# Ternarising the weights in steps of 2048 columns with bf16 intermediates instead of 512 columns with f32

## The chip, the cores and the metric

The kernel runs on all 8 NeuronCores of one Trainium2 chip. Each core computes one sequence of a batch of eight, with the same program and its own copy of the weight preparation; the cores exchange nothing. The metric is the device time of the slowest core in microseconds. Engine names as in the profile: PE is TensorE, DVE VectorE, ACT ScalarE, POOL GpSimd, SP the engine that here only issues loads.

## What is computed

One layer of a "sandwich" network on x of shape (8, 4096, 2048), f32: linear attention with 16 heads and 4 key/value heads, then a feed-forward block with ternary weights (BitLinear 1.58).

```python
def weight_quant(w):
    scale = 1.0 / jnp.clip(jnp.mean(jnp.abs(w)), 1e-05)
    q = jnp.clip(jnp.round(w * scale), -1.0, 1.0) / scale
    return w + jax.lax.stop_gradient(q - w)
def bitlinear158(x, w, b):
    xq = act_quant(rms_norm(x))
    wq = weight_quant(w)
    return jnp.einsum('bsd,od->bso', xq, wq) + b

x = x + _layernorm(attn(_layernorm(x), Wq, bq, Wk, bk, Wv, bv, Wo))
# ffn: w1 is (8192, 2048), w2 is (2048, 8192)
#   h = layer_norm(gelu(silu(bitlinear158(x, w1, b1)))); bitlinear158(h, w2, b2)
x = x + _layernorm(ffn(_layernorm(x), w1, b1, ln_g, ln_b, w2, b2))
```

The part that matters here is `weight_quant`: each element of w1 and w2 becomes -1, 0 or 1 once it is multiplied by the scale and rounded, and the scale needs the mean of |w| over the whole matrix first.

## The kernel before

The program is a list of operations per engine, written out by hand; semaphores order them. `vo`, `so`, `po` append an operation to VectorE, ScalarE and GpSimd, `vs` one that also waits for the VectorE operation before it. `dma(queue, ...)` (L157 to L164; the profile puts issues down to L162) appends a transfer to the queue of SP ("sync"), ACT ("scalar") or POOL ("gpsimd"). Each queue has a ring of semaphores, six for SP and three each for ACT and POOL, and a transfer waits until the one that used its semaphore before has landed.

It has two parts. The token loop (from L446) works on 8 tiles of 512 tokens: attention passes over all tiles and then the feed-forward block. The weight preparation in front of it casts the attention weights to bf16, and then handles w1 and w2 one after the other (`for wi, wsrc` at L330), each in two passes over chunks of 128 rows of the transposed matrix:

- The first pass (L333 to L346) loads each chunk to `xf` and sums the absolute values on VectorE. From the sum follows the scale, as a column `swc` (L347 to L365).
- The second pass (L367 to L410), the ternarisation, loads each chunk again and compares: `v_u` (L378) is 1 where w times scale is over 0.5, `v_w` (L384) is 1 where it is under -0.5, and `v_q` (L389) is the difference, in bf16. Then the chunk is stored to HBM, from where the token loop reads it.

A chunk of w1 has 8192 columns and fills all of `xf`: 16 chunks, each load waiting until VectorE is done with the chunk before. It is stored with one transfer of 2 MB to `wq1d` on ACT's queue. A chunk of w2 has 2048 columns, and two halves of `xf` alternate: 64 chunks, so that a load can be issued two chunks ahead. It is stored as 16 pieces of 128 columns to `wq2d`, 8 on ACT's queue and 8 on POOL's. The result buffer is `yb` for even chunks and `sqs` for odd ones, and the first `v_q` of a chunk waits for the last six stores of the chunk two before it (`st_prev`).

The inner loop of the second pass takes 512 columns at a time. `tA(0)` and `tA(1)` are the halves of `tmpA`, 512 f32 columns each; `rot_auxp` makes each comparison wait for the subtraction that last read its half. `xb1` is a bf16 buffer of 8192 columns which the preparation doesn't use; the token loop does. The load of the first tokens waits for all stores of the preparation (`pre_store`).

Of the kernel before, what the change touches and what calls it, by code (L numbers as in the profile page):

```python
# [63 lines left out]
def build_nc(debug=False):  # L64
# [37 lines left out]
    with es:  # L102
        A1 = SB("A1", [128, 32768], BF16)
        A2 = SB("A2", [128, 16384], BF16)
        xf = SB("xf", [128, DC * T], F32)
        yb = SB("yb", [128, DC * T], BF16)
        sqs = SB("sqs", [128, DC * T], BF16)
        xb1 = SB("xb1", [128, DC * T], BF16)
# [77 lines left out]
        vo = lambda fn, waits=(), inc=None: sch.op("vector", fn, waits, inc)  # L186
# [12 lines left out]
        tA = lambda i: tmpA[:, (i % 2) * 512:(i % 2) * 512 + 512]  # L199
        tB = lambda i: tmpB[:, 0:512]  # L200
        aux = lambda i: aux32[:, (i % 2) * 512:(i % 2) * 512 + 512]
        chunk = lambda t, c, w=512: t[:, c * w:(c + 1) * w]
# [34 lines left out]
        def bcast(rowslice, bank, dest, bf16, row_w=()):  # L237
# [7 lines left out]
            else:  # L245
# [30 lines left out]
           waits=[c_bk, c0])  # L276
# [4 lines left out]
                   waits=[W("v", vlast)] + qlast("sync"))  # L281
        slast2 = 0
        for c in range(DC):
            if c % 2 == 0:
                vlast = vo(lambda e, c=c: e.tensor_copy(out=chunk(A2, c),
                                                        in_=chunk(xf, c)),
                           waits=[c_wk] if c == 0 else (),
                           inc="v" if c >= DC - 2 else None)
            else:
                slast2 = so(lambda e, c=c: e.copy(out=chunk(A2, c),  # L290
                                                  in_=chunk(xf, c)),
                            waits=[c_wk] if c == 1 else (),
                            inc="s" if c >= DC - 2 else None)
        c_wv = dma("sync", xf[:].rearrange("p (c o) -> p c o", c=16), wvT.rearrange("(c p) o -> p c o", p=128),
                   waits=[W("v", vlast), W("s", slast2)])
        for c in range(DC):
            if c % 2 == 0:
                vlast = vo(lambda e, c=c: e.tensor_copy(
                    out=A2[:, 8192 + c * 512:8192 + (c + 1) * 512],
                    in_=chunk(xf, c)),  # L300
                    waits=[c_wv] if c == 0 else (),
                    inc="v" if c >= DC - 2 else None)
            else:
                slast2 = so(lambda e, c=c: e.copy(
                    out=A2[:, 8192 + c * 512:8192 + (c + 1) * 512],
                    in_=chunk(xf, c)),
                    waits=[c_wv] if c == 1 else (),
                    inc="s" if c >= DC - 2 else None)
        slast = sch.at("s")
        vlast = sch.at("v")  # L310
        for q4 in range(4):
            src = wqT[q4 * 512:(q4 + 1) * 512, :].rearrange("(c p) o -> p c o",
                                                            p=128)
            c_l = dma("sync", xf[:].rearrange("p (c o) -> p c o", c=4), src, waits=[W("v", vlast), W("s", slast)])
            for c in range(4):
                dc = q4 * 4 + c
                if c % 2 == 0:
                    vlast = vo(lambda e, dc=dc, c=c: e.tensor_copy(
                        out=A1[:, dc * 2048:(dc + 1) * 2048],
                        in_=xf[:, c * 2048:(c + 1) * 2048]),  # L320
                        waits=[c_l], inc="v")
                else:
                    slast = so(lambda e, dc=dc, c=c: e.copy(
                        out=A1[:, dc * 2048:(dc + 1) * 2048],
                        in_=xf[:, c * 2048:(c + 1) * 2048]),
                        waits=[c_l], inc="s")

        rot_auxp = Rot(2)
        rot_wst = Rot(2)
        for wi, wsrc in enumerate((w1T, w2T)):  # L330
            nch = DC if wi == 0 else MC
            wid = HID if wi == 0 else D
            for ch in range(nch):  # L333
                off = 0 if wid == HID else (ch % 2) * 4096
                c_l = dma("sync", xf[:, off:off + wid], wsrc[ch * 128:(ch + 1) * 128, :],
                          waits=(rot_wst.wait(ch) if wid != HID else
                                 [W("v", sch.at("v"))]) +
                                ([W("v", sch.at("v")), W("s", sch.at("s"))]
                                 if ch < 2 else []))
                vs(lambda e, wid=wid, off=off: e.reduce_sum(  # L340
                    out=wacc[:, 2:3], in_=xf[:, off:off + wid], axis=AX.X,
                    apply_absolute_value=True), waits=[c_l])
                va = vs(lambda e, wi=wi: e.tensor_tensor(  # L343
                    out=wacc[:, wi:wi + 1], in0=wacc[:, wi:wi + 1],
                    in1=wacc[:, 2:3], op=OP.add))
                rot_wst.done(ch, "v", va)  # L346
            t_tp = tpose(psp[0:1, 0:128], wacc[:, wi:wi + 1], idf[:],  # L347
                         waits=[W("v", sch.at("v"))] + guard(psp), inc="pe")
            vs(lambda e: e.tensor_reduce(out=wrow[0:1, 0:1], in_=psp[0:1, 0:128],
                                         axis=AX.X, op=OP.add),  # L350
               waits=[W("pe", t_tp)])
            vs(lambda e: e.tensor_scalar(out=wrow[0:1, 1:2], in0=wrow[0:1, 0:1],
                                         scalar1=1.0 / float(D * HID), scalar2=1e-5,
                                         op0=OP.mult, op1=OP.max))
            vs(lambda e: e.reciprocal(out=wrow[0:1, 2:3], in_=wrow[0:1, 1:2]))
            v_sw = vs(lambda e, wi=wi: e.tensor_scalar(
                out=wrow[0:1, 4 + wi:5 + wi], in0=wrow[0:1, 1:2],
                scalar1=1.0 / 127.0, scalar2=None, op0=OP.mult))
            consumed(psp, "v", v_sw)
            t_bc = mm(psp[:, 0:1], onesrf[0:1, :], wrow[0:1, 2:3], True, True,  # L360
                      waits=[W("v", v_sw)] + guard(psp), inc="pe")
            v_swc = vs(lambda e, wi=wi: e.tensor_copy(out=swc[:, wi:wi + 1],
                                                      in_=psp[:, 0:1]),
                       waits=[W("pe", t_bc)])
            consumed(psp, "v", v_swc)  # L365
            st_prev = {0: [], 1: []}
            for ch in range(nch):  # L367
                off = 0 if wid == HID else (ch % 2) * 4096
                wbuf = yb if ch % 2 == 0 else sqs
                c_l = dma("sync", xf[:, off:off + wid],  # L370
                          wsrc[ch * 128:(ch + 1) * 128, :],
                          waits=(rot_wst.wait(ch) if wid != HID else
                                 [W("v", sch.at("v"))]) +
                                ([W("v", sch.at("v"))] if ch < 2 else []) +
                                (qlast("scalar") + qlast("gpsimd")
                                 if ch < 2 else []))
                for j in range(wid // 512):
                    v_u = vo(lambda e, j=j, wi=wi, off=off: e.tensor_scalar(  # L378
                        out=tA(0), in0=xf[:, off + j * 512:off + (j + 1) * 512],
                        scalar1=swc[:, wi:wi + 1],  # L380
                        scalar2=0.5, op0=OP.mult, op1=OP.is_gt),
                        waits=([c_l] if j == 0 else []) + rot_auxp.wait(0),
                        inc="v")
                    v_w = vo(lambda e, j=j, wi=wi, off=off: e.tensor_scalar(  # L384
                        out=tA(1), in0=xf[:, off + j * 512:off + (j + 1) * 512],
                        scalar1=swc[:, wi:wi + 1],
                        scalar2=-0.5, op0=OP.mult, op1=OP.is_lt),
                        waits=rot_auxp.wait(1), inc="v")
                    v_q = vo(lambda e, j=j, wbuf=wbuf: e.tensor_tensor(  # L389
                        out=chunk(wbuf, j), in0=tA(0), in1=tA(1), op=OP.subtract),  # L390
                        waits=[W("v", v_w)] +
                              (st_prev[ch % 2] if j == 0 else []), inc="v")
                    rot_auxp.done(0, "v", v_q)
                    rot_auxp.done(1, "v", v_q)
                m_v = sch.at("v")
                if wid != HID:
                    rot_wst.done(ch, "v", m_v)
                if wi == 0:
                    st_prev[ch % 2] = [dma("scalar",
                                           wq1d[ch * 128:(ch + 1) * 128, :],  # L400
                                           wbuf[:, 0:HID],
                                           waits=[W("v", m_v)])]
                else:
                    sts = []
                    for jc in range(DC):
                        q = "scalar" if jc % 2 == 0 else "gpsimd"
                        sts.append(dma(q, wq2d[jc, ch * 128:(ch + 1) * 128, :],
                                       wbuf[:, jc * 128:(jc + 1) * 128],
                                       waits=[W("v", m_v)] if jc < 2 else ()))
                    st_prev[ch % 2] = sts[-6:]  # L410
        if debug:
            v_dbg = vo(lambda e: e.tensor_copy(out=tcol[:, 0:4], in_=wacc[:]),
                       waits=[W("v", sch.at("v"))], inc="v")
            v_dbg = vo(lambda e: e.tensor_copy(out=tcol[:, 4:8], in_=swc[:]),
                       inc="v")
# [30 lines left out]
        for i in range(NT):  # L446
            c_x = dma("sync", xf[:].rearrange("p (c t) -> p c t", c=DC),
                      xT[:, i * T:(i + 1) * T].rearrange("(c p) t -> p c t", p=128),
                      waits=xf_free)
            pe_sq = 0  # L450
            for c in range(DC):
                v_xb = vo(lambda e, c=c: e.tensor_copy(out=xb_sl(c),  # L452
                                                       in_=chunk(xf, c)),
                          waits=([c_x] if c == 0 else []) + rot_xb.wait(c),
                          inc="v")
                s_sq = so(lambda e, c=c: e.activation(out=sq_sl(c), in_=xb_sl(c),  # L456
                                                      func=AF.Square),
                          waits=[W("v", v_xb)] + rot_sq.wait(c), inc="s")
                mm(pst0[0:1, :], onesb[:, 0:1], xb_sl(c), c == 0, c == DC - 1,
                   waits=[W("v", v_xb)] + (guard(pst0) if c == 0 else []))  # L460
                pe_sq = mm(pst1[0:1, :], onesb[:, 0:1], sq_sl(c), c == 0, c == DC - 1,
                           waits=[W("s", s_sq)] + (guard(pst1) if c == 0 else []),
                           inc="pe")
# [7 lines left out]
            for c in range(DC):  # L471
                v_t1 = vo(lambda e, c=c: e.scalar_tensor_tensor(
                    out=tA(c), in0=chunk(xf, c), scalar=1.0, in1=bcA[:, :],
                    op0=OP.bypass, op1=OP.mult),
                    waits=([W("s", s_bA)] if c == 0 else []) + rot_tA.wait(c) +
                          (yb_free if c == 0 else []), inc="v")
                fn = lambda e, c=c: e.tensor_tensor(
                    out=chunk(yb, c), in0=tA(c), in1=bcB[:, :], op=OP.subtract)
# [13 lines left out]
            for s_ in range(4):  # L492
                g = s_ % 2
                for c in range(DC):
# [6 lines left out]
                          inc="pe")  # L501
# [110 lines left out]
        for i in range(NT):  # L612
# [77 lines left out]
            for c in range(DC):  # L690
# [4 lines left out]
                    inc="v")  # L695
# [514 lines left out]
```

How the kernel before makes its waits and increments, by code:

```python
            def body(e):  # L1150
                for ws, fn, inc, amt in sch.q[eng_name]:
                    for (sem, val) in ws:
                        e.wait_ge(sem, val)
                    if fn is not None:
                        inst = fn(e)
                        if inc is not None and inst is not None:
                            inst.then_inc(inc, amt)
```

## Time and profile before

| | us |
|---|---|
| two timed runs | 16645.35 and 16755.38, median 16700.36 |
| the profiled execution | 16641.38 |
| its span on the slowest core (core 2) | 16639.8 |
| spans of the eight cores | 16567.9 to 16639.8 |
| VectorE busy | 6066.2 (36%) |
| TensorE matmuls busy | 6774.4 (41%) |
| GpSimd busy | 1518.0 (9%) |
| HBM read / written | 964.91 MB / 150.99 MB |

All rows are of core 2 in the profiled execution, in microseconds from the start of its span. "Busy" counts instructions on an engine, not the time in which it waits. A wait is put down to the instruction or transfer that released it last. The issue of a transfer by SP or ACT stands under SPq and ACTq and isn't counted as busy; POOL's issues are, since that engine's cores write the descriptors.

### The profile page before, as it was taken

The page shows a single profiled execution, that of the slowest core. Times are in us where ns is not written, and L with a number is a line of the kernel's source. Part 1 is how long each engine was busy: PE and PEld are TensorE (multiplying, and loading weights), DVE is VectorE, ACT ScalarE, POOL GpSimd, SP SyncE. Part 2 cuts the span into 40 slices and gives each one's busy share as a digit, 9 for nine tenths or more (in the row PEclk, how much of TensorE's full clock was granted, in tenths as well). Part 3 has the DMA queues.
Part 4 walks back from the last instruction along what each step waited for, and adds up shares of the span by engine and source line. Part 5 has one row for each costly group of instructions (what it writes and reads, how often), then busy time and mean ns, then how long its engine had stood idle before and what let it go on. Part 6 is the DMA issues. An engine that isn't in the chain of part 4 may idle for free.

```text
span 16639.8 us, 99990 instructions; the slowest of 8 cores (16567.9 to 16639.8 us)
## 1 busy us (share of the span) xinstructions
PE 6774.4 (41%) x25302; PEld 2496.0 (15%) x25302; DVE 6066.2 (36%) x10104; ACT 3165.0 (19%) x4923; POOL 1518.0 (9%) x1476
## 2 busy tenths in 40 slices
PE   0000057745454361661553345156155244515615
PEld 0000022311111120220220112022022011102202
DVE  3555644511111226225234432522523433352252
ACT  0000011112121132032122113203202211320320
POOL 0001410000000010001001001000100100100110
PEclk9999987866666675785775667578577567757857
DMA  5336521121101120430330222033033022203303
GB/s 200 139 136 211 153 67 46 36 74 38 51 26 51 36 76 0 96 86 0 71 91 21 46 69 68 5 91 86 0 71 97 14 51 71 61 12 84 86 0 81
DMA packets 1033539, 1122.40 MB, mean 67 GB/s; under 512 B 92818, under 2 KB 912146, under 8 KB 1006356
## 3 DMA queue, kind: packets, MB, share of 16 engines
q1 hardware_dynamic: 891028, 964.94, 20.6%
q10 hardware_dynamic: 125568, 134.25, 2.4%
q0 software_dynamic: 16384, 16.81, 0.3%
q8 instruction: 221, 3.62, 0.1%
q14 instruction: 338, 2.77, 0.1%
HBM read 964.91 MB, written 150.99 MB: 67 GB/s over the span
## 4 chain that ended last, share of the span: by engine, by line
PE 34%; DVE 25%; issue 12%; DMA 11%; ACT 9%; POOL 7%; DVEq 1%; ACTq 0%; POOLq 0%; SPq 0%
PE pmm L176 20%; PE pkvA L176 8%; PE pst L176 5%; POOL tmpB L984 4%; DMA xf<-w1T 3%; DVE tmpA L766 3%; ACT pst L752 3%; DVE tmpA L757 3%; DVE tmpB L761 3%; ACT aux L749 2%; DVE tmpB L1057 2%; DVE tmpA L979 2%; PE psp L176 2%; DVE A L770 1%; DVE wacc L340 1%
## 5 line engine op out<-in xcount | busy, mean ns | idle before, releaser
L176 PE MATMUL pmm<-A 128*128 128x512 bf16 x5632 | 1453.4, 406 | 2477.1 <-DVE A L770 2477.1
L176 PE MATMUL pmm<-yb,A 128*128 128x512 bf16 x8320 | 1925.8, 390 | 41.9 <-DMA A<-wq1d 20.8
L176 PE MATMUL pst<-sqs,onesb 128*1 128x512 bf16 x1536 | 752.0, 492 | 1971.1 <-ACT sqs L1002 1109.4
L176 PEld LDWEIGHTS pmm<-A 128*128 128x128 bf16 x5632 | 556.1, 100 | 3368.7 <-issue 2803.8
L176 PEld LDWEIGHTS pmm<-yb,A 128*128 128x128 bf16 x8320 | 819.2, 100 | 1110.3 <-issue 286.1
L984 POOL TENSOR_TENSOR tmpB<-tmpA,bcB 128x512 f32<-128x512 f32 x512 | 646.0, 1262 | 3148.2 <-ACT bcB L248 2409.8
L757 DVE SCALAR_TENSOR_TENSOR tmpA<-tmpB,pst 128x512 f32<-128x512 f32 x640 | 440.2, 688 | 1351.6 <-ACT pst L752 1351.6
L749 ACT ACTIVATE aux<-tmpB 128x512 int32<-128x512 f32 x640 | 402.6, 629 | 2627.5 <-DVE tmpB L1057 1988.0
L176 PE MATMUL pst<-rows,onesrf 1*128 1x512 f32 x320 | 317.6, 1104 | 1151.0 <-DVE yb L770 858.8
L176 PE MATMUL pkvA<-yb,A 128*128 128x512 bf16 x3328 | 760.0, 382 | 20.5 <-DMA A<-wq1d 19.4
L1128 POOL TENSOR_TENSOR tmpB<-tmpA,bcB 128x512 f32<-128x512 f32 x128 | 161.4, 1261 | 5619.9 <-ACT bcB L248 5426.5
L176 PE MATMUL pst<-xb,onesb 128*1 128x512 bf16 x512 | 196.2, 428 | 1066.6 <-DVE xb L452 720.3
L940 DVE SCALAR_TENSOR_TENSOR tmpA<-pmm,bcA 128x512 f32<-128x512 f32 x344 | 237.5, 692 | 1029.7 <-PE pmm L176 893.2
L183 PE MATMUL psp<-idf,wacc 128*1 128x128 f32 x2 | 0.7, 371 | 1489.6 <-DVE wacc L343 1489.6
L946 ACT ACTIVATE A<-tmpA,b1c 128x512 bf16<-128x512 f32 x512 | 364.7, 720 | 1157.5 <-DVE tmpA L940 1157.1
L989 DVE TENSOR_SCALAR A<-tmpB,gc,bbc 128x512 bf16<-128x512 f32 x512 | 279.6, 546 | 816.5 <-POOL tmpB L984 816.5
L176 PE MATMUL pkvA<-A 128*128 128x512 bf16 x2560 | 572.4, 386 | 0.0
L1091 DVE SCALAR_TENSOR_TENSOR tmpA<-pmm,bcB 128x512 f32<-128x512 f32 x88 | 60.9, 692 | 1279.8 <-PE pmm L176 1279.8
L1002 ACT ACTIVATE sqs<-A 128x512 bf16<-128x512 bf16 x512 | 322.4, 630 | 1075.4 <-DVE A L989 1075.4
L176 PEld LDWEIGHTS pst<-sqs,onesb 128*1 128x1 bf16 x1536 | 121.8, 79 | 2637.4 <-issue 2636.8
L223 DVE TENSOR_TENSOR rows<-rows 1x512 f32<-1x512 f32 x40 | 27.2, 679 | 1252.9 <-ACT rows L219 1252.9
L456 ACT ACTIVATE xb<-xb 128x512 bf16<-128x512 bf16 x128 | 79.6, 628 | 2118.5 <-DVE xb L452 2115.0
(182 smaller groups left out, 10022.0 us busy)
## 6 DMA issues: line engine op xcount, KB each, us to landing
A<-wq1d SPq DMA_DIRECT2D x256, 1024.0 KB, 6.3
xf<-w1T SPq DMA_DIRECT2D x32, 4096.0 KB, 13.0
xf<-w2T SPq DMA_DIRECT2D x128, 1024.0 KB, 5.2
xf<-xT SPq DMA_DIRECT2D x16, 4096.0 KB, 14.5
xnTd<-xf ACTq DMA_DIRECT2D x8, 4096.0 KB, 15.2
xf<-xnTd SPq DMA_DIRECT2D x8, 4096.0 KB, 14.8
outT<-xf ACTq DMA_DIRECT2D x8, 4096.0 KB, 12.3
xf<-wqT SPq DMA_DIRECT2D x4, 4096.0 KB, 14.1
```

The lines of the kernel that those rows point to most:

```text
L176: lambda e: e.matmul(out=out, lhsT=lhsT, rhs=rhs, start=start, stop=stop, skip_group_check=True),
L749: if False else e.activation(out=aux(c), in_=tsrc, func=AF.Identity),
L752: s_rf = so(lambda e, g=g: e.activation(out=pstb[g][:, 0:512], in_=aux(c), func=AF.Identity, bias=epsc[:, 3:4]), waits=[W("s", s_c1)] + gu ...
L757: v_d = vo(lambda e, g=g: e.scalar_tensor_tensor(out=tA(c), in0=tsrc, scalar=-1.0, in1=pstb[g][:, 0:512], op0=OP.add, op1=OP.subtract), wa ...
L761: v_r1 = vo(lambda e, g=g: e.scalar_tensor_tensor(out=tsrc, in0=tA(c), scalar=0.5, in1=pstb[g][:, 0:512], op0=OP.is_gt, op1=OP.add), waits ...
L766: v_r2 = vo(lambda e: e.scalar_tensor_tensor(out=tA(c), in0=tA(c), scalar=-0.5, in1=tsrc, op0=OP.is_ge, op1=OP.add), waits=[W("v", v_r1)], ...
L946: s_sis[oc] = so(lambda e, oc=oc: e.activation(out=chunk(A1, oc), in_=tA(oc), func=AF.Silu, bias=b1c[:, oc:oc + 1]), waits=[W("v", v_ds)], ...
L979: v_l1 = vo(lambda e, m=m: e.scalar_tensor_tensor(out=tA(m), in0=chunk(A1, m), scalar=1.0, in1=bcAb[:, :], op0=OP.bypass, op1=OP.mult), wa ...
L984: p_l2 = po(lambda e, m=m: e.tensor_tensor(out=tB(m), in0=tA(m), in1=bcB[:, 0:512], op=OP.subtract), waits=[W("v", v_l1)] + ([W("s", s_bB4 ...
L989: v_l3s[m] = vo(lambda e, m=m: e.tensor_scalar(out=chunk(A1, m), in0=tB(m), scalar1=gc[:, m:m + 1], scalar2=bbc[:, m:m + 1], op0=OP.mult, ...
L1002: s_q5 = so(lambda e, m=m: e.activation(out=hq_sl(m), in_=chunk(A1, m), func=AF.Square), waits=[W("v", v_l3s[m])] + rot_sq.wait(m), inc="s")
L1057: v_z1 = vo(lambda e, m=m: e.scalar_tensor_tensor(out=tB(m), in0=chunk(A1, m), scalar=1.0, in1=bcAb[:, :], op0=OP.bypass, op1=OP.mult), wa ...
```

## The change

In the second pass the inner loop takes 2048 columns at a time: four rounds for a chunk of w1 and one for a chunk of w2. The two comparisons write to the first and second 2048 columns of `xb1`, in bf16, instead of the two halves of `tmpA` in f32, and the subtraction reads them there and writes 2048 columns of the result buffer. The waits are the same ones, once per group of three instructions. Loads, stores and everything else stay.

```diff
--- before.py
+++ after.py
@@ -374,22 +374,25 @@
                                 ([W("v", sch.at("v"))] if ch < 2 else []) +
                                 (qlast("scalar") + qlast("gpsimd")
                                  if ch < 2 else []))
-                for j in range(wid // 512):
-                    v_u = vo(lambda e, j=j, wi=wi, off=off: e.tensor_scalar(
-                        out=tA(0), in0=xf[:, off + j * 512:off + (j + 1) * 512],
+                for j2 in range(wid // 2048):
+                    o2 = off + j2 * 2048
+                    v_u = vo(lambda e, o2=o2, wi=wi: e.tensor_scalar(
+                        out=xb1[:, 0:2048], in0=xf[:, o2:o2 + 2048],
                         scalar1=swc[:, wi:wi + 1],
                         scalar2=0.5, op0=OP.mult, op1=OP.is_gt),
-                        waits=([c_l] if j == 0 else []) + rot_auxp.wait(0),
+                        waits=([c_l] if j2 == 0 else []) + rot_auxp.wait(0),
                         inc="v")
-                    v_w = vo(lambda e, j=j, wi=wi, off=off: e.tensor_scalar(
-                        out=tA(1), in0=xf[:, off + j * 512:off + (j + 1) * 512],
+                    v_w = vo(lambda e, o2=o2, wi=wi: e.tensor_scalar(
+                        out=xb1[:, 2048:4096], in0=xf[:, o2:o2 + 2048],
                         scalar1=swc[:, wi:wi + 1],
                         scalar2=-0.5, op0=OP.mult, op1=OP.is_lt),
                         waits=rot_auxp.wait(1), inc="v")
-                    v_q = vo(lambda e, j=j, wbuf=wbuf: e.tensor_tensor(
-                        out=chunk(wbuf, j), in0=tA(0), in1=tA(1), op=OP.subtract),
+                    v_q = vo(lambda e, j2=j2, wbuf=wbuf: e.tensor_tensor(
+                        out=wbuf[:, j2 * 2048:(j2 + 1) * 2048],
+                        in0=xb1[:, 0:2048], in1=xb1[:, 2048:4096],
+                        op=OP.subtract),
                         waits=[W("v", v_w)] +
-                              (st_prev[ch % 2] if j == 0 else []), inc="v")
+                              (st_prev[ch % 2] if j2 == 0 else []), inc="v")
                     rot_auxp.done(0, "v", v_q)
                     rot_auxp.done(1, "v", v_q)
                 m_v = sch.at("v")
```

## Rows read from the trace of the kernel before

**Rows 1.** Page, the span in 40 slices, busy tenths of DVE and of the DMA engines

```profile
DVE  3555644511111226225234432522523433352252
...
DMA  5336521121101120430330222033033022203303
```

**Rows 2.** Stretches: busy us of PE, PEld, DVE, ACT, POOL, TensorE clock, DMA share, GB/s

```profile
475.00:1222.00 747.00, 0.00 (x0) 0.00 (x0) 403.49 (x768) 0.00 (x0) 0.00 (x0) 1.00 0.33 132
...
1500.00:2176.00 676.00, 0.00 (x0) 0.00 (x0) 406.45 (x768) 0.00 (x0) 285.53 (x512) 1.00 0.49 148
...
2176.00:16640.00 14464.00, 6772.53 (x25296) 2494.88 (x25296) 4939.65 (x8360) 3140.40 (x4898) 1232.22 (x960) 0.69 0.20 53
```

**Rows 3.** Chain of work that ended last, by line, 1500 to 2176 us

```profile
by line: DMA wq2d<-sqs 30.3%; DMA wq2d<-yb 26.5%; issue 15.5%; DVE sqs L389 7.9%; DVE tmpA L384 7.3%; DVE yb L389 5.4%; DVE tmpA L378 2.6%; POOL wq2d L162 2.5%; DMA xf<-w2T 0.9%; DVEq L1153 0.7%; POOLq L1153 0.3%; ACTq L162 0.2%; ACTq L1153
```

**Rows 4.** Timeline of one w1 chunk: start us, us, engine, line, operation [idle before]

```profile
1175.62 0.33 SPq L162 DMA_DIRECT2D xf<-w1T  x1
...
1193.37 0.48 DVE L378 TENSOR_SCALAR tmpA<-xf,swc 128x512 f32<-128x512 f32 x1 [17.88 <-DMA xf<-w1T]
...
1195.22 0.49 DVE L378 TENSOR_SCALAR tmpA<-xf,swc 128x512 f32<-128x512 f32 x1
1195.62 0.48 DVE L384 TENSOR_SCALAR tmpA<-xf,swc 128x512 f32<-128x512 f32 x1
1196.21 0.69 DVE L389 TENSOR_TENSOR sqs<-tmpA 128x512 bf16<-128x512 f32 x1
1197.01 0.49 DVE L378 TENSOR_SCALAR tmpA<-xf,swc 128x512 f32<-128x512 f32 x1
...
1222.08 0.33 SPq L162 DMA_DIRECT2D xf<-w2T  x1
```

**Rows 5.** DVE instructions by line and shape, whole span: busy us, mean ns, idle before

```profile
L1018 DVE TENSOR_TENSOR sqs<-sqs,A 128x512 bf16<-128x512 bf16 x504 | 219.5, 436 | 0.5
...
L378 DVE TENSOR_SCALAR tmpA<-xf,swc 128x512 f32<-128x512 f32 x512 | 251.3, 491 | 363.0 <-DMA xf<-w1T 290.3 <-DMA xf<-w2T 19.2 <-DVE sqs L389 0.5
...
L384 DVE TENSOR_SCALAR tmpA<-xf,swc 128x512 f32<-128x512 f32 x512 | 246.9, 482 | 0.0
...
L389 DVE TENSOR_TENSOR yb<-tmpA 128x512 bf16<-128x512 f32 x256 | 177.3, 692 | 114.9 <-DMA wq2d<-yb 48.4 <-DMA wq2d<-sqs 33.2 <-DVE tmpA L384 10.6
...
L340 DVE TENSOR_REDUCE wacc<-xf 128x1 f32<-128x2048 f32 x64 | 146.3, 2286 | 106.6 <-DMA xf<-w2T 106.6
...
L1098 DVE TENSOR_SCALAR xb<-tmpA,b2c 128x512 bf16<-128x512 f32 x128 | 62.2, 486 | 15.1 <-DVE tmpA L1091 2.4
...
L318 DVE CAST A<-xf 128x2048 bf16<-128x2048 f32 x8 | 9.4, 1223 | 61.3 <-DMA xf<-wqT 61.3
...
L285 DVE CAST A<-xf 128x512 bf16<-128x512 f32 x8 | 2.8, 422 | 19.0 <-DMA xf<-wkT 19.0
```

**Rows 6.** Waits of POOL, 1500 to 2176 us: us in total, times, longest

```profile
POOL wq2d L162 <- DMA wq2d<-sqs: 161.4, 82, 4.8
...
POOL wq2d L162 <- DMA wq2d<-yb: 132.2, 72, 4.7
...
POOL wq2d L162 <- DVE tmpA L378: 53.3, 29, 15.2
...
POOL wq2d L162 <- issue: 22.7, 40, 6.8
```

**Rows 7.** Timeline of one round of two chunks in the w2 pass

```profile
1907.77 0.69 DVE L389 TENSOR_TENSOR yb<-tmpA 128x512 bf16<-128x512 f32 x1 [5.76 <-DMA wq2d<-yb]
...
1913.93 0.49 DVE L378 TENSOR_SCALAR tmpA<-xf,swc 128x512 f32<-128x512 f32 x1
...
1914.42 1.60 POOL L162 DMA_DIRECT2D wq2d<-yb  x3 [1.14 <-DVE tmpA L378]
...
1920.29 1.80 POOL L162 DMA_DIRECT2D wq2d<-yb  x3 [4.28 <-DMA wq2d<-yb]
...
1928.09 0.69 DVE L389 TENSOR_TENSOR yb<-tmpA 128x512 bf16<-128x512 f32 x1 [5.72 <-DMA wq2d<-yb]
```

## Prediction

> **What bounds the kernel now.** The busy strip of the page comes first [rows 1]. Each digit is a fortieth of the span, 416 us. In the first five slices, up to about 2,180 us, only VectorE (DVE) and the DMA engines work to speak of; TensorE starts in the sixth. So the weight preparation stands alone in front of everything and every microsecond of it that is really on its own path is a microsecond of the span. The change touches only two passes of it. The table of stretches gives their lengths [rows 2]: the ternarisation of w1 from 475 to 1,222 us (747 us, DVE busy 403) and that of w2 from 1,500 to 2,176 us (676 us, DVE busy 406, POOL busy 286 with 512 store issues). The remaining 14,464 us run the token loop, none of whose instructions changes.
>
> The second question is what each pass waits for, and the two passes differ. In the w1 pass the timeline [rows 4] shows one chunk: the load is issued at 1175.62, the first comparison starts at 1193.37 after 17.88 us of idle DVE, and the next load is issued at 1222.08. Load and arithmetic alternate strictly: 17.8 us of load plus 28.7 us of DVE make 46.5 us, and 16 such chunks make the 747 us. The store of a chunk travels while the next one is loaded and the buffer is needed again only two chunks later, so it delays nothing but the load that it shares the DMA engines with. Here DVE time counts in full.
>
> In the w2 pass it does not. The chain of work [rows 3] goes for 57% (30.3 + 26.5) through the stores to `wq2d` and for 23% (7.9 + 7.3 + 5.4 + 2.6) through the three DVE lines. The waits of POOL [rows 6] say more. Its own share of the stores, 8 per chunk, is busy for 286 us, waits 161.4 + 132.2 = 293.6 us for landings of its earlier stores (each queue has three semaphores, so store n waits for n-3), 53.3 us for DVE, and 22.7 us are "issue". Together 656 of 676 us: POOL's queue is close to full whatever DVE does. The timeline [rows 7] shows why the landings are slow. The even chunk's stores start at 1914.42, together with the next load; the second set of three can go only at 1920.29, 5.9 us later, and the buffer is free at 1928.09, 14.2 us after the chunk was finished at 1913.9. DVE then runs the waiting subtraction and three more groups, and the round begins again: 1928.09 - 1907.77 = 20.3 us for two chunks, 32 such rounds.
>
> **The change part by part.** *Removed:* in each pass 256 groups of three instructions on 512 columns. From the starts [rows 4] a group takes 1197.01 - 1195.22 = 1.79 us: 0.40 from the first comparison to the second, 0.59 to the subtraction, 0.80 to the next group. The durations are 0.49, 0.48 and 0.69 [rows 4, 5]; the first two overlap by 0.09 and the other two are followed by 0.11 us each, the wait for the instruction before.
>
> *Added:* in each pass 64 groups on 2048 columns, with bf16 in between. No row of before has such a comparison, so I build it. What a further column costs a one-source DVE instruction follows from the two sizes of the cast: (1223 - 422) / 1536 = 0.521 ns [rows 5]. 1536 more columns add 0.80 us. That the comparison may now write bf16 costs nothing: the same operation with f32 in and bf16 out takes 486 ns at L1098, as the f32 one does at L378 (491) and L384 (482) [rows 5]. So the intervals become 0.40 + 0.80 = 1.20 and 0.59 + 0.80 = 1.39 us. The subtraction gains twice. With f32 inputs a 512-column one takes 692 ns, with bf16 in and out 436 ns (L1018) [rows 5]; the second at 2048 columns, again with 0.80 added, is 1.24 us, and with the 0.11 of wait 1.35. A new group is 1.20 + 1.39 + 1.35 = 3.94 us against 4 x 1.79 = 7.16, a gain of 3.2 us per 2048 columns. Bounds: if bf16 inputs brought the subtraction nothing at this width, it would take what the slowest DVE row at that width takes, 2.29 us (the f32 sum at L340) [rows 5], and the group 4.99. At the other end, if all three ran at their part of the cast's rate with no fixed time, 3 x 1.07 = 3.2 us.
>
> *w1 pass:* a chunk has four new groups, 15.8 us instead of 28.6. 16 chunks x 12.85 = 206 us. All of it is on the path. The load and the store it travels with keep their 17.8 us; the DMA engines are busy 33% of this pass [rows 2], which becomes 45%, so at most a microsecond per load (16 us) could be lost if cores come into each other's way.
>
> *w2 pass:* a chunk is one new group, so after the wait for the buffer only one subtraction of 1.35 us remains instead of 20.3 - 14.2 = 6.1 us. Lower bound of the gain: 0, if POOL's queue stays as full as it is. Upper bound: (6.1 - 1.35) x 32 = 152 us, if the stores still take 14.2 us from their start and the round shrinks to 15.6 us. But POOL must fit 16 stores into each round, and its 18.1 us per round of issue and landing waits ((286 + 293.6) / 32) do not depend on DVE. What a faster DVE takes away for certain is POOL's waiting for DVE: 53.3 us, of which 15.2 is one wait at the second chunk that is mostly a load; I keep its 3.2 us share, and 3.2 more before the very first store, and get 53.3 - 15.2 + 6.4 = 45 us. Of the 22.7 us of "issue" (6.8 of it in one piece) another 10 or so should go with fewer DVE instructions in the way. I take 55 us, near the queue's bound and not the 152, because the queue's row covers 97% of the pass.
>
> *Moved:* the temporaries go from `tmpA` to `xb1`, which nothing uses before the token loop; the loop's first write of it is by DVE itself. No DMA and no queue order changes. The pass ends, as now, with about 8 us of stores and then the load of the first tokens (14.6 us), both unchanged.
>
> *Sum:* 206 + 55 = 261 us. The profiled execution took 16641.4 us (span 16639.8), so 16380 for one like it. The two timed runs were 16645 and 16755, median 16700, 59 us above the profiled one; the fast end is what two of the three show, so I add only 10 and say 16390.
>
> **The rivals.**
>
> *Rival 1, POOL and the DMA engines absorb it.* The w2 pass is bound by stores and loads only, and DVE's speed-up moves the loads into more stores' way. For it: the full queue [rows 6]. Against: the 53 us of waits for DVE. Time: 16641 - 206 = 16435, rounded 16440.
>
> *Rival 2, the loop from buffer to buffer sets the pace.* The stores' 14.2 us stay, the round becomes 15.6 us. For it: the last wait of each round is DVE's for the buffer, 5.7 us [rows 7], and the chain has 23% of DVE (157 us) [rows 3]. Against: 16 POOL stores would have to go in 15.6 us where they need 18.1 now. Time: 16641 - 206 - 152 = 16283.
>
> *Rival 3, the wide comparisons hold up POOL's stores.* POOL's first stores of a chunk are issued 0.45 us after the chunk's end, just when DVE begins the next chunk's two comparisons, now 2.6 us long together. If POOL is held until they end, it loses up to 2.1 us a chunk, 64 x 2.1 = 134 us. Time: 16380 + 134 = 16515. For it: 22.7 us of short "issue" gaps on POOL beside DVE work. Against: at 1914.42 three stores are issued in 1.60 us, 0.53 each, right under two comparisons and a subtraction [rows 7]. The Trainium skill has a rule for this (SBUF — State Buffer, "SBUF: two separate sides"): while VectorE runs an instruction that uses both ports, GpSimd is locked out and cannot write the descriptors of its DMAs. By that rule the sum would be Rival 3's; the 0.53 us per issue in rows 7 does not show it, at instructions of 0.5 us.
>
> *Rival 4, the subtraction stays slow at 2048 columns.* Then the w1 pass gains 64 x (7.16 - 4.99) = 139 us, the w2 pass still about 50. Time: 16641 - 189 = 16452. L1018's 436 ns speaks against it.
>
> *Rival 5, slower: every set of stores meets a load.* With DVE ahead, a load might be in flight whenever a set of three POOL stores is. Each set would take 5.9 us instead of the 3.8 of now (20.3 us / 5.33 sets), a round 31.4 us, the pass 32 x 11.1 = 355 us more, and the total 16641 - 206 + 355 = 16790. It decides from 206 / 32 = 6.4 us more per round, 5.0 us per set. Against: there are only two loads of some 5 us in a round.
>
> **How the numbers follow.** Forecast (w1 in full, w2 by POOL's queue, 16350 to 16430): 0.52. Rival 1: 0.14. Rival 2 or a part-way gain below 16350: 0.17. Rival 3: 0.08. Rival 4: 0.06. Rival 5: 0.03. The range 16280 to 16500 holds the forecast, rivals 1, 2 and 4, and the 110 us by which timed runs differ for most of them; out are rival 3, 5 and slow repeats of rivals 1 and 4. Two per cent of 16700, about what a measurement of this kernel can tell from no change, is 334 us, so the line lies at 16366, just under the forecast. Faster by over 2%: rival 2 and a quarter of the forecast, 0.30. Slower: hardly rival 5, 0.02. Within: 0.68.
>
> **What would show it.** DVE comparisons of 2048 columns near 1.29 us and subtractions near 1.24; w1 chunks 33.6 us apart, the pass 541 us; loads there still near 18 us. In the w2 pass rounds of about 18.6 us, POOL waiting for DVE hardly at all, its waits for landings still near 290 us, and DVE waiting for stores for most of the pass. The token loop 14,464 us, give or take 30. I am wrong if subtractions take over 2 us (rival 4), if POOL's issues grow or gaps called "issue" exceed 100 us (rival 3), or if landing waits shrink by 100 us (rival 2) or grow (1, 5).

## The result and the profile after

| | before | changed kernel |
|---|---|---|
| median of the timed runs, us | 16681.18 (10 runs) | 16439.08 (11 runs) |
| lowest and highest | 16590.34 to 16755.38 | 16359.93 to 16475.93 |
| ratio to before, 95% interval | | 0.9851, 0.9827 to 0.9876 |

The interval is a gain of 207 to 289 us on 16681. The next table splits it. Each entry is the median over the eight cores of the profiled execution, read from the issue of the first load of the next stage or from the TensorE instruction that closes a first pass.

| stage, us | before | changed kernel | difference |
|---|---|---|---|
| up to the ternarisation of w1 | 471.9 | 475.3 | +3.4 |
| ternarisation of w1 | 743.6 | 539.4 | -204.2 |
| first pass over w2 | 271.8 | 271.8 | 0 |
| ternarisation of w2 | 684.0 | 656.3 | -27.7 |
| token loop | 14419.8 | 14468.6 | +48.8 |

The two passes that the change touches give 232 us. The token loop has the same instructions in both; in the eleven kernels below it took 14410 to 14476 us in single executions, and nothing here ties its 49 us to the change.

The stretches of the slowest core of the changed kernel (bounds, length, busy us of PE, PEld, DVE, ACT and POOL, TensorE clock, DMA share, GB/s) answer to [rows 2]:

```profile
484.00:1026.00 542.00, 0.92 (x3) 0.58 (x3) 238.06 (x199) 0.00 (x0) 0.00 (x0) 1.00 0.46 182
...
1297.00:1952.00 655.00, 0.93 (x3) 0.58 (x3) 238.56 (x198) 0.00 (x0) 347.18 (x512) 1.00 0.51 154
...
1952.00:16439.00 14487.00, 6729.05 (x24824) 2493.90 (x25296) 4939.40 (x8360) 3140.21 (x4898) 1232.29 (x960) 0.69 0.20 53
```

DVE is busy 238 us instead of 403 and 406 in each pass. POOL issues the same 512 stores, but is busy 347 us instead of 286. The DVE instructions by line and shape (busy us, mean ns, idle before), which answer to [rows 5]:

```profile
L379 DVE TENSOR_SCALAR xb<-xf,swc 128x2048 bf16<-128x2048 f32 x128 | 165.0, 1289 | 322.6 <-DMA xf<-w1T 289.1 <-DMA xf<-w2T 21.8
...
L385 DVE TENSOR_SCALAR xb<-xf,swc 128x2048 bf16<-128x2048 f32 x128 | 163.8, 1280 | 0.0
...
L390 DVE TENSOR_TENSOR yb<-xb 128x2048 bf16<-128x2048 bf16 x64 | 78.4, 1225 | 191.6 <-DMA wq2d<-sqs 102.0 <-DMA wq2d<-yb 85.1 <-DVE xb L385 1.7
...
L390 DVE TENSOR_TENSOR sqs<-xb 128x2048 bf16<-128x2048 bf16 x64 | 78.4, 1225 | 189.6 <-DMA wq2d<-yb 117.8 <-DMA wq2d<-sqs 67.9 <-DVE xb L385 1.2
```

A comparison of 2048 columns takes 1.29 and 1.28 us and a subtraction 1.23. The timeline of the last w1 chunk, beside [rows 4]:

```profile
1010.74 1.28 DVE L379 TENSOR_SCALAR xb<-xf,swc 128x2048 bf16<-128x2048 f32 x1 [17.78 <-DMA xf<-w1T]
1011.95 1.28 DVE L385 TENSOR_SCALAR xb<-xf,swc 128x2048 bf16<-128x2048 f32 x1
1013.40 1.23 DVE L390 TENSOR_TENSOR sqs<-xb 128x2048 bf16<-128x2048 bf16 x1 [0.17 <-DVE xb L385]
1014.73 1.29 DVE L379 TENSOR_SCALAR xb<-xf,swc 128x2048 bf16<-128x2048 f32 x1
...
1026.52 0.35 ACTq L162 DMA_DIRECT2D wq1d<-sqs  x1
1026.56 49.76 SPq L162 DMA_DIRECT2D xf<-w2T  x11
```

The group takes 1014.73 - 1010.74 = 3.99 us here, with 0.17 us of wait at its first subtraction, and 3.92 in the other three; the chunk is over 15.8 us after its load landed, and the load itself took 17.8 us.

In the w2 pass POOL's waits (us in total, times, longest), beside [rows 6]:

```profile
POOL wq2d L162 <- DMA wq2d<-yb: 132.2, 79, 4.7
...
POOL wq2d L162 <- DMA wq2d<-sqs: 130.0, 70, 4.0
...
POOL wq2d L162 <- issue: 15.7, 10, 6.3
...
POOL wq2d L162 <- DVE sqs L390: 12.9, 1, 12.9
```

and the chain of work that ended last in this pass, beside [rows 3]:

```profile
by line: DMA wq2d<-yb 39.2%; DMA wq2d<-sqs 36.4%; issue 15.7%; POOL wq2d L162 5.5%; DMA xf<-w2T 1.8%; POOLq L1156 0.6%; DVE xb L385 0.4%; DVE sqs L390 0.2%; DVE yb L390 0.2%; DVE swc L362 0.0%; SPq L1156 0.0%; DVEq L1156 0.0%; DVE xb L379 0
```

POOL hardly waits for DVE any more: 12.9 us, in one piece at the second chunk, instead of 53.3. DVE's lines, 23% of the chain before, are under 1%. But stores to `wq2d` are now 76% of it instead of 57%. The timeline of half a round, beside [rows 7]:

```profile
1705.60 1.22 DVE L390 TENSOR_TENSOR sqs<-xb 128x2048 bf16<-128x2048 bf16 x1 [5.89 <-DMA wq2d<-sqs]
1706.03 4.03 POOL L162 DMA_DIRECT2D wq2d<-yb  x5 [0.69 <-DMA wq2d<-sqs]
1706.93 1.29 DVE L379 TENSOR_SCALAR xb<-xf,swc 128x2048 bf16<-128x2048 f32 x1
1706.95 10.32 SPq L162 DMA_DIRECT2D xf<-w2T  x2
...
1708.13 1.28 DVE L385 TENSOR_SCALAR xb<-xf,swc 128x2048 bf16<-128x2048 f32 x1
1713.77 0.54 POOL L162 DMA_DIRECT2D wq2d<-yb  x1 [3.71 <-DMA wq2d<-yb]
1714.32 1.07 POOL L162 DMA_DIRECT2D wq2d<-sqs  x2
1715.59 1.23 DVE L390 TENSOR_TENSOR yb<-xb 128x2048 bf16<-128x2048 bf16 x1 [6.18 <-DMA wq2d<-yb]
```

The subtraction waits 5.9 us for its buffer, and 1.35 us later the load for two chunks ahead is issued (1706.95). POOL's five stores from 1706.03 on take 4.03 us where 5 x 0.54 = 2.7 would do, with both comparisons beside them. Here is one of the five, and the comparison beside it, taken alone:

```profile
1706.93 1.29 DVE L379 TENSOR_SCALAR xb<-xf,swc 128x2048 bf16<-128x2048 f32 x1
...
1707.09 1.25 POOL L162 DMA_DIRECT2D wq2d<-yb  x1
```

This issue ends at 1708.34, 0.12 us after the comparison, which ends at 1708.22. On every core 106 to 116 of the 512 issues take over 0.7 us, and each of them ends 0.12 us after a comparison does (0.115 to 0.128). The 69 to 74 issues per core that run beside the subtraction alone, which has 2048 columns too, take 0.54 us. After the five stores the next one goes at 1713.77, 3.7 us later, once a store that went beside the load has landed. A chunk comes every 10.0 us here, where in [rows 7] it was 10.2; over the pass it is 656.3 / 64 = 10.3 against 10.7.

Both POOL's and ACT's queue carry stores of every chunk, and a subtraction waits for the last three of each. POOL's set the pace: in 488 of the 496 cases (62 chunks on eight cores) the subtraction waited, and the last landing before it was POOL's. ACT's last store of a chunk had landed 9.4 us after the chunk's end in the median, POOL's 18.4 us after it.

### The profile page after: what moved, and what is told of

Read it like the earlier page. It is cut to its first block, busy times and chain, and to the rows that moved or that the text cites. A ratio compares the mean times of both kernels' runs of the same rounds, so it can differ in the third digit from the quotient of the medians.

```text
span 16439.6 us, 97214 instructions; the slowest of 8 cores (16340.1 to 16439.6 us)
## 1 busy us (share of the span) xinstructions
PE 6730.9 (41%) x24830; PEld 2495.1 (15%) x25302; DVE 5730.8 (35%) x8952; ACT 3164.8 (19%) x4923; POOL 1579.7 (10%) x1476
## 4 chain that ended last, share of the span: by engine, by line
PE 34%; DVE 23%; DMA 12%; issue 12%; ACT 10%; POOL 7%; DVEq 1%; ACTq 0%; POOLq 0%; SPq 0%
PE pmm L176 20%; PE pkvA L176 8%; PE pst L176 5%; POOL tmpB L987 4%; DMA xf<-w1T 3%; DVE tmpA L769 3%; ACT pst L755 3%; DVE tmpA L760 3%; DVE tmpB L764 3%; ACT aux L752 2%; DVE tmpB L1060 2%; DVE tmpA L982 2%; DMA wq2d<-yb 2%; PE psp L176 2%; DMA wq2d<-sqs 1%
## 5 line engine op out<-in xcount | busy, mean ns | idle before, releaser
L1107 ACT ACTIVATE sqs<-xb 128x512 bf16<-128x512 bf16 x128 | 80.6, 630 | 2027.3 <-DVE xb L1101 2027.3
L769 DVE SCALAR_TENSOR_TENSOR tmpA<-tmpA,tmpB 128x512 f32<-128x512 f32 x640 | 442.8, 692 | 68.2 <-DVE tmpB L764 1.8
```

Source lines behind the costliest of these rows:

```text
L769: v_r2 = vo(lambda e: e.scalar_tensor_tensor(out=tA(c), in0=tA(c), scalar=-0.5, in1=tsrc, op0=OP.is_ge, op1=OP.add), waits=[W("v", v_r1)], ...
```

## The experiments

The questions: does each pass give what the table says by its own loop; what of it is the width and what the type; and why did the w2 pass give 28 us and not 55. For the last, theory A was that POOL's queue sets the pace and that the wide comparisons hold its issues up on the path. Theory B was that the landings of stores beside loads set it, and that the longer issues lie in slack. All stage times are medians over the cores of one profiled execution. POOL's columns are its time within the w2 pass: busy with issues, waiting for landings, and waiting for DVE after its first store.

| kernel | w1 pass | w2 pass | POOL busy | landings | for DVE | total |
|---|---|---|---|---|---|---|
| before | 743.6 | 684.0 | 285.5 | 297.1 | 61.8 | 16681 |
| changed | 539.4 | 656.3 | 349.1 | 263.9 | 11.3 | 16439 |
| e1, w1 only | 538.1 | 680.7 | 285.0 | 296.8 | 60.6 | 16444 |
| e2, w2 only | 745.5 | 653.6 | 347.9 | 260.4 | 11.6 | 16659 |
| e3, bf16 at 512 | 673.8 | 673.4 | 288.5 | 312.2 | 33.9 | 16570 |
| e4, narrow comparisons | 588.3 | 645.1 | 295.2 | 289.2 | 12.1 | 16465 |
| e5, rings of eight | 536.7 | 446.1 | 329.5 | 58.0 | 32.3 | 16207 |
| e6, POOL's stores by SP | 536.2 | 891.1 | 0 | 0 | 0 | 16672 |
| e7, no loads in w2 | 536.4 | 481.6 | 351.8 | 82.3 | 10.9 | 16242 |
| e8, halves | 344.6 | 653.6 | 349.4 | 258.9 | 11.4 | 16097 |
| e9, halves and rings | 345.9 | 451.2 | 329.8 | 62.0 | 32.2 | 15916 |
| e10, before with rings | 742.1 | 516.6 | 292.9 | 0 | 196.4 | 16473 |
| e11, e9 with narrow comparisons in w2 | 347.8 | 435.3 | 310.8 | 40.2 | 63.3 | 15886 |

The totals of e1 to e8 and e10 are single runs, and runs of one kernel differ by over 100 us, so their verdicts are read from the stages.

**e1 and e2: one pass each.** e1 runs the old inner loop for w2 and the new one for w1, e2 the reverse (e1 against the changed kernel, shortened):

```diff
-                for j2 in range(wid // 2048):
+                for j2 in range(wid // 2048 if wi == 0 else 0):
+                    ...                       # new group
+                for j in range(wid // 512 if wi == 1 else 0):
+                    ...                       # old group
```

> Only the w1 pass has the wide bf16 loop; w2 keeps 512 columns and f32. Every theory: w1 pass 541 us as in the changed kernel (744 before), w2 pass 684 us as before with POOL's 512 issues busy 286 us and some 55 us of POOL waiting for DVE. Total about 204 us under before. If instead the w2 pass comes out near 656 us here too, its 27 us don't come from its own loop.

> Only the w2 pass has the wide bf16 loop. Every theory: w1 pass 744 us, w2 pass about 656 us, POOL's 512 issues busy about 347 us, total about 27 us under before, less than the spread of single runs, so the pass is read from the trace.

Both came out as expected: 538.1 and 680.7 us in e1, 745.5 and 653.6 us in e2. The two gains are separate and each belongs to its own loop. e2 as a whole, 16659 us against 16628 in the single run of before beside it, shows nothing by itself.

**e3: the type alone.** The groups stay at 512 columns, the intermediates go to `xb1` in bf16:

```diff
-                        out=tA(0), in0=xf[:, off + j * 512:off + (j + 1) * 512],
+                        out=xb1[:, 0:512], in0=xf[:, off + j * 512:off + (j + 1) * 512],
...
-                        out=chunk(wbuf, j), in0=tA(0), in1=tA(1), op=OP.subtract),
+                        out=chunk(wbuf, j), in0=xb1[:, 0:512], in1=xb1[:, 512:1024], op=OP.subtract),
```

> All three instructions at 512 columns, only the intermediates are bf16: what the type alone brings. Group 0.40 + 0.59 + 0.55 = 1.54 us instead of 1.79, w1 pass 744 - 256 x 0.25 = 680 us. w2 pass: chunk 6.2 us instead of 7.2. Theory A (POOL's queue): issues busy 286 us, POOL waits for DVE some 30 us instead of 53, pass 655 to 665. Theory B (landings): no further than 675 to 684.

The w1 pass took 673.8 us: the type gives 70 of the 204 us, the width, on top of it, the other 134. The w2 pass took 673.4, between the two forecasts and nearer to B's: POOL waits 28 us less for DVE, as A had it, and 15 us more for landings.

**e4: narrow comparisons, wide subtraction.** It takes the long comparisons away and leaves the rest:

```diff
+                    for k in range(4):
                         v_u = vo(lambda e, ...: e.tensor_scalar(
-                        out=xb1[:, 0:2048], in0=xf[:, o2:o2 + 2048],
+                            out=xb1[:, k * 512:(k + 1) * 512],
+                            in0=xf[:, o2 + k * 512:o2 + (k + 1) * 512],
```

> The comparisons go back to 512 columns (bf16 out), the subtraction stays at 2048. In the w2 pass all comparisons of a chunk lie before the wait for the buffer, so DVE's part after the wait is the same 1.3 us. Theory A (wide comparisons hold up POOL's issues, and POOL's queue sets the pace): POOL's 512 issues are busy 286 to 295 us again instead of 347, and the w2 pass falls from 656 us towards 600 to 620. Theory B (landings beside the loads set the pace, the longer issues lie in slack): POOL busy falls the same way but its landing waits grow by as much, and the pass stays within 10 us of 656. w1 pass in both: a group takes 4 x 0.99 + 1.34 = 5.3 us, the pass 541 + 64 x 1.36 = 628 us.

The trace of its slowest core: POOL's store issues (ns least/median/most), and what POOL waited for (us, times).

```profile
L162 POOL DMA_DIRECT2D wq2d<-yb x256: 537/537/827, 1373.8 to 1996.7; - x128
...
  DMA wq2d<-yb: 156.3, 97
...
  DMA wq2d<-sqs: 136.9, 72
...
  issue: 24.3, 37
```

and the same row of the changed kernel:

```profile
L162 POOL DMA_DIRECT2D wq2d<-yb x256: 537/537/1537, 1309.9 to 1942.8; - x128
...
L162 POOL DMA_DIRECT2D wq2d<-sqs x256: 537/537/1582, 1328.7 to 1949.9; - x128
```

No issue takes more than 0.83 us when the comparisons are narrow; with the wide ones some take up to 1.58. So the wide comparisons do hold the issues up, at 349.1 - 295.2 = 54 us over the pass. But the pass became only 11 us shorter: landing waits rose by 25 us, and gaps called "issue" by 11. At 645.1 us it lies one microsecond outside theory B's range and 25 above theory A's, so with three semaphores per queue theory B is much the nearer one. The w1 pass took 588.3 us, not the 628 forecast: I had given each pair of comparisons 0.99 us, up to the subtraction behind it, while in this trace a pair followed by another comparison goes every 0.80.

**e5: rings of eight.**

```diff
-        QR = {"sync": 6, "scalar": 3, "gpsimd": 3}
+        QR = {"sync": 6, "scalar": 8, "gpsimd": 8}
```

> The changed kernel with eight semaphores instead of three for the queues of ACT and POOL, so a store no longer waits for the third one before it. If the pace of the w2 pass (656 us) is set by waits for landings one after another (264 us of POOL's time), they go: POOL keeps its 347 us of issue, each set of eight meets its load once, and the pass comes down to 450 to 520 us. If the DMA engines themselves can't move the data faster beside the loads, it stays over 600 us.

The w2 pass fell from 656.3 to 446.1 us, just under the forecast. What POOL waited for in the pass (us, times), and how long its stores took to land:

```profile
  DMA wq2d<-yb: 37.1, 39
...
  DMA wq2d<-sqs: 21.0, 17
...
DMA to landing us min/median/max: 1.7/4.6/7.5
```

The single store lands later than before, after 4.6 us in the median (1.9 in the kernel before, 1.8 in the changed one), but POOL's landing waits are down to 58 us from 264, since eight stores may be in flight. The wait for the third store before was what turned slow landings into time. The edit deepens ACT's ring too. No run separates the two; that POOL's stores land last in the changed kernel speaks for POOL's.

**e6: POOL's stores on SP's queue.**

```diff
-                        q = "scalar" if jc % 2 == 0 else "gpsimd"
+                        q = "scalar" if jc % 2 == 0 else "sync"
```

> The changed kernel with POOL's half of the w2 stores issued by SP, between its loads, with its ring of six; POOL issues nothing. Theory A (POOL's queue sets the pace): 349 us of issue and its landings go, the pass falls to 520 to 580 us, where ACT's queue with eight stores per chunk and a ring of three becomes the limit (about 8 us per chunk). Theory B (any store that meets a load waits for the load): still 5 to 6 us for a set beside a load, but two sets of six and two instead of three, three and two; the pass 560 to 630 us.

It missed both forecasts: the w2 pass took 874 to 904 us on the eight cores, and the total was 16671.7. The timeline shows a mistake in the design (start us, us, queue or engine, operation, idle before):

```profile
1711.96 3.95 SPq L162 DMA_DIRECT2D wq2d<-yb  x8
1716.07 0.33 SPq L162 DMA_DIRECT2D xf<-w2T  x1
1722.38 1.28 DVE L379 TENSOR_SCALAR xb<-xf,swc 128x2048 bf16<-128x2048 f32 x1 [10.56 <-DMA xf<-w2T]
```

SP works through its queue in order. The load for the next chunk stands behind the eight stores of this one, so it is issued at 1716.07 when they are out, and DVE waits 10.6 us for it. What had been a load two chunks ahead became a load on the path. Between theory A and B this run decides nothing.

**e7: no loads beside the stores.**

```diff
-                c_l = dma("sync", xf[:, off:off + wid],
+                c_l = None if (wi == 1 and ch >= 2) else dma(
+                          "sync", xf[:, off:off + wid],
```

> Leaves out the loads of the w2 ternarisation after the first two chunks (the later chunks are computed from the same data), so the stores meet no load. If the landings are slow because of the loads: POOL's landings take 1.8 to 2.3 us each, its landing waits fall from 264 us to under 120, and the pass is POOL's own issue plus that, 440 to 480 us. If stores are slow by themselves the pass stays over 600 us.

The kernel leaves out these loads and so computes wrong values for w2; it serves for its times alone. The pass took 481.6 us, just over the forecast, and the landing times of POOL's stores (us least/median/most) were

```profile
DMA to landing us min/median/max: 1.7/1.7/3.5
```

where the changed kernel has 1.7/1.8/6.8. Without loads no store of this core lands later than 3.5 us, POOL's landing waits fall from 264 to 82 us, and its 352 us of issue are then most of the pass.

**e8: w1 in halves.** Both w1 passes load 4096 columns at a time into the two halves of `xf`, each half as soon as DVE has left it:

```diff
+                    c_ls = [dma("sync", xf[:, h * 4096:(h + 1) * 4096],
+                                wsrc[ch * 128:(ch + 1) * 128,
+                                     h * 4096:(h + 1) * 4096],
+                                waits=rot_wst.wait(h) + first)
+                            for h in range(2)]
...
+                    if wid == HID and j2 % 2 == 1:
+                        rot_wst.done(j2 // 2, "v", v_q)
```

> The changed kernel with both w1 passes loading half a chunk (4096 columns) at a time into the two halves of the buffer, so that a load runs beside the arithmetic on the other half. What is shown if the 18 us of load now stands alone on the path: the ternarisation of w1 falls from 539 us to the DMA time of 16 chunks, 16 x 18 = 290 to 320 us, and the first w1 pass from 16 x 21.6 to 16 x 12.5 us, 145 us less. Total 16439 - 235 - 145 = about 16060 us. If two loads in flight with a store only slow each other down, the ternarisation stays over 450 us.

The ternarisation of w1 took 344.6 us instead of 539.4, a chunk every 21.5 us instead of 33.7. That is above the 290 to 320 us forecast, and more than the 18 us of one load; what takes the other 3.5 us a chunk was not separated. Load and arithmetic together took 33.6 us, so most of the load is now hidden. The part before it fell from 475 to 352 us, 124 us and not the 145 forecast. The total was 16097.0.

**e9, e10, e11.**

> Halves for w1 and rings of eight together, on top of the changed kernel. The two gains lie in different passes and should add: first w1 pass and ternarisation of w1 as with halves (345 us instead of 539), w2 pass 446 us instead of 656. Total 16439 - 120 - 194 - 210 = 15915 us, ratio to before 0.955.

It took 15916.0 us against 16653.1 beside it, ratio 0.9566 (0.9543 to 0.9590). The gains add: the stages came out at 345.9 us for w1 (345 forecast) and 451.2 for w2 (446). That the total lies within a microsecond of the forecast is in part luck, since the four runs spread over 41 us and the w2 pass alone is 5 us off.

e10 changes only the ring line, in the kernel before:

> The kernel before with rings of eight: narrow f32 loop, deep rings. It tells what the new loop is worth in the w2 pass once landings no longer set the pace. If DVE is then the limit, the pass takes 64 x 7.2 = 461 us plus the waits for loads, 480 to 520 us, so that the new loop would be worth 35 to 75 us there instead of 27. If the DMA engines set the pace of both, it is 446 us like the wide loop with rings of eight.

The pass took 516.6 us. So the new loop is worth 517 - 446 = 71 us in the w2 pass with deep rings, within the forecast of 35 to 75, where it was worth 28 with shallow ones. Now POOL has no landing waits at all and waits for DVE instead (us in total, times, longest):

```profile
POOL wq2d L162 <- DVE tmpA L378: 191.1, 61, 13.8
```

e11 narrows the comparisons of the w2 pass again, in e9:

> As the kernel with halves and rings of eight, but in the w2 pass the comparisons have 512 columns again (the subtraction 2048). With shallow rings this gave POOL 54 us of issue time back and the pass only 11. Theory A (POOL's longer issues lie on the path once the rings are deep): POOL busy 330 to 290 us and the pass 10 to 40 us shorter than 446. Theory B (they lie in slack): the pass the same within 10 us, or longer by part of the 64 x 0.8 = 49 us that the narrower comparisons cost DVE.

The w2 pass took 435.3 us instead of 451.2, the total 15886.1, ratio 0.9543 (0.9524 to 0.9562). The stretches around the w2 pass on the slowest core of e9 and then of e11, in the columns of the stretches above; the third busy time is DVE's, the fifth POOL's:

```profile
970.00:1440.00 470.00, 0.93 (x3) 0.58 (x3) 243.30 (x201) 0.00 (x0) 327.83 (x512) 1.00 0.76 223
```

```profile
980.00:1440.00 460.00, 0.92 (x3) 0.57 (x3) 297.13 (x589) 0.00 (x0) 309.85 (x512) 1.00 0.79 230
```

DVE is busy 54 us longer, POOL 18 us less, and the pass is 16 us shorter: theory A's sign and the low end of its size, with deep rings. The 16 us are not the issues alone: by the medians POOL's landing waits fell by 22 us as well, and its waits for DVE rose by 31. The whole kernels' intervals overlap, so at the total this is open; e11 is the fastest kernel here, with e9 not told apart from it.

## Why the prediction was right, and where it was not

**The DVE terms held.** The comparison built from the cast's slope came out at 1.29 and 1.28 us (expected 1.29), the subtraction at 1.23 (1.24), the group at 3.92 to 3.99 (3.94).

**The w1 term held.** 206 us were predicted, 204 measured, and e1 has it alone. DVE's waits for the loads of this pass went from 283.8 to 286.4 us (median over the cores; 17.4 to 20.0 us for every chunk but the first), though the DMA share rose from 33% to 46%. So of the 16 us that might have been lost there, 3 were.

**The w2 term was mis-sized: 55 us predicted, 28 measured.** The step that failed is the sentence that POOL's 18.1 us of issue and landing waits per round "do not depend on DVE". The part that does depend on DVE went about as forecast, 45 us: POOL's wait for DVE fell from 61.8 to 11.3 us by the medians, and the time before the first store by another 3. But issue rose by 64 us, landing waits fell by 33 and gaps by 5, where the prediction had 0, 0 and 10. So issue and landing waits together went from 18.2 to 19.2 us per round. The queue's time shrank by about 25 us in all, with the 3 before the first store the 28 of the pass. That the issues would lengthen was rival 3's mechanism, priced at 134 us at most and given 0.08. It did occur, at half the size, and growing issues are one of the signs by which the prediction wanted to be called wrong. e4 shows that it cost little: of 54 us given back to POOL, 36 went into landing waits and gaps, and the pass gained 11. So the long issues explain 11 of the 27 us that are missing from the 55. The other 16 are missing in e4 as well, where against the kernel before issues took 10 us more, 9 of them beside comparisons, and gaps 6 us more, not 10 less; why the gaps grew was not tested. The rule I had set aside was the better guide to POOL's busy time: the Trainium skill (SBUF — State Buffer, "SBUF: two separate sides") has GpSimd locked out while VectorE runs a two-port instruction, and in the traces the longest issue goes from 0.79 us beside comparisons of 0.49 us to 1.58 us beside ones of 1.29, and each long one ends just behind a comparison. The lockout is not for the whole of both comparisons: the five stores above lost 1.3 us beside 2.5 us of them. The [rows 7] from which I argued against it had stores beside short comparisons only.

**Which of the other rivals occurred.** Rival 1's description of the w2 pass (stores and loads set the pace) was right as far as it went: e7 without loads and e5 with more stores in flight each take 175 to 210 us off, while e4 takes 11. Its price, no gain at all, was wrong: the pass gained 28 us. Rival 2 fell: DVE left the chain, but its place went to landings. The rival needed the time from a chunk's end to the next use of its buffer to stay at 14.2 us; it went from 14.4 to 18.6 us (median over the pass and the cores), and the round from 20.5 only to 19.8. Rivals 4 and 5 fell on the 1.23 us subtraction and on landing waits that went down.

**The total.** The predicted gain was 261 us on the profiled execution, the measured ratio makes it 249 us on 16681, and the passes themselves show 232. The forecast of 16390 was 49 us under the median of 16439. Of that, 30 us are the reference: I had stayed near the fast end of three runs (16641, plus 10), and the median of ten is 16681. The other 19 are gain: 242 us between the two medians, not 261. By the stages the gain was short by 29, nearly all of it in the w2 term; the 10 us between these figures are less than the runs differ among themselves.

## What to carry to other kernels

Ask first whether the engine alternates with its load or works beside it: in the first case its time counts one for one, in the second look at the queue that is nearly full and at what each of its items waits for. And when the wait for one thing goes away, do not assume that the queue's other terms stay as they are. A ring of only three semaphores turned slow landings into waiting here; one line was worth 210 us in the w2 pass, nearly as much as the rewritten loop in both (232), and loading in halves 318. And when an instruction is made longer, look for who is held up while it runs, here GpSimd's store issues, also if the total of that engine's work goes down.

## What the runs showed of the hardware

- POOL's issue of a 32 KB store took 0.54 us alone and up to 1.58 us beside a 2048-column comparison from f32 to bf16; over 512 issues, 64 us more. The long issues ended 0.12 us after the end of a comparison. Beside 512-column comparisons an issue took at most 0.84 us on any core, and beside the 2048-column subtraction of two bf16 inputs (1.23 us) it stayed at 0.54.
- POOL's stores landed after up to 6.8 us where 1 MB loads ran, without such loads after 3.5 us at most, 1.7 in the median (slowest cores). On the eight cores of the changed kernel 1936 stores of POOL's and ACT's queue were issued while a load on SP's queue was in flight, and all of them landed after the load, on the slowest core 0.7 us after it in the median. With rings of eight 97% still did (4813 of 4953).
- In the w1 pass bf16 intermediates saved 70 of 744 us, and three instructions on 2048 columns instead of twelve on 512 another 134. The type is worth 0.27 us a group, where the 692 and 436 ns of [rows 5] differ by 0.26.
